# Attention in an eight-core transformer layer: the probability-times-value product, turned around and woven into the scores

## The reference

```python
x = x + attn(layernorm(x), ...)          # layernorm again inside, Wq, Wkv, Wout
#   q: 16 heads of 64, k and v: 4 groups of 64; q and k get a layernorm per head
#   attn = softmax(q k^T / 8); out = attn v; out @ Wout
x = x + ffn(layernorm(x), w1, w2)        # 1024 -> 4096 -> 1024, exact gelu,
#   ternary weights, activations quantized to 8 bits per token
```

## Time and profile before

| | |
|---|---|
| median of 3 runs | 9662.07 us (9659.97 to 9666.74) |
| profiled execution | 9662.5 us |
| its span on the slowest core (core 2) | 9661.0 us (all cores: 9604.8 to 9661.0) |
| TensorE busy | 4180.0 us, 43% |
| VectorE busy | 3207.8 us, 33% |
| ScalarE busy | 1954.3 us, 20% |
| mean granted TensorE clock | 0.595 |
| attention core of the two sequences | 1366.2 and 1367.0 us |

### The profile page before, as it was taken

The page is one execution under the profiler, slowest core; times in us unless marked ns, Lnnn a source line. Parts: engine busy times, 40 slices in busy tenths (PEclk is TensorE's granted clock), DMA queues, the critical chain, the costliest instruction groups (busy, mean ns, idle before and its releaser), DMA issues.

```text
span 9661.0 us, 60136 instructions; the slowest of 8 cores (9604.8 to 9661.0 us)
## 1 busy us (share of the span) xinstructions
PE 4180.0 (43%) x19456; PEld 1636.5 (17%) x19456; DVE 3207.8 (33%) x5038; ACT 1954.3 (20%) x2197; POOL 0.2 (0%) x4
## 2 busy tenths in 40 slices
PE   4233656666664365666665200222212222015445
PEld 0000211222221121222222100111101111002222
DVE  0423131111111322111111377655566555660000
ACT  1012203434342211434433111000000000001111
POOL 0000000000000000000000000000000000000000
PEclk8675755555556665555555555666556666557777
DMA  4232000000001100000000100111101111022221
GB/s 156 89 128 79 11 0 1 1 1 1 1 3 52 50 0 0 1 1 1 1 1 24 57 28 29 37 52 52 50 22 33 52 52 52 31 76 70 70 67 53
DMA packets 199070, 358.72 MB, mean 37 GB/s; under 512 B 23257, under 2 KB 154718, under 8 KB 194674
## 3 DMA queue, kind: packets, MB, share of 16 engines
q1 hardware_dynamic: 198770, 354.87, 11.3%
HBM read 279.29 MB, written 75.50 MB: 37 GB/s over the span
## 4 chain that ended last, share of the span: by engine, by line
PE 38%; DVE 30%; ACT 14%; issue 8%; DMA 6%; SPq 3%; DVEq 1%; ACTq 0%
ACT pslab L768 6%; PE ps_PV L778 6%; PE ps_S L757 5%; PE ps_F L1210 5%; PE ps_F L1086 4%; PE pss L267 3%; PE ps_qn L735 3%; PE ps_W L835 2%; DVE hflt L1138 2%; DVE htile L1133 2%; DVE hflt L1134 2%; DVE hflt L1136 2%; PE ps_mu L611 2%; DVE colmisc L1117 1%; DVE ao_tm L790 1%
## 5 line engine op out<-in xcount | busy, mean ns | idle before, releaser
L757 PE MATMUL ps_S<-qt,kt 65*128 65x512 bf16 x2048 | 985.2, 611 | 278.8 <-ACT pslab L768 242.3
L768 ACT ACTIVATE pslab<-ps_S 128x1024 bf16<-128x1024 f32 x1024 | 994.8, 1021 | 152.1 <-PE ps_S L757 150.2
L1149 PE MATMUL ps_trH<-s_idb,hqtm 128*128 128x128 bf16 x1024 | 129.5, 307 | 1541.1 <-DVE colmisc L1142 1439.4
L1210 PE MATMUL ps_F<-hqin,w2tb 128*128 128x512 bf16 x2048 | 499.3, 406 | 561.4 <-DMA f2xst<-scr_x 430.6
L788 DVE RECIPROCAL colmisc<-ps_PV 128x1 f32<-128x1 f32 x512 | 86.1, 168 | 1948.7 <-PE ps_PV L778 1948.7
L778 PE MATMUL ps_PV<-vaug,pslab 128*128 128x65 bf16 x8192 | 531.5, 242 | 453.2 <-DVE ao_tm L790 365.4
L778 PEld LDWEIGHTS ps_PV<-vaug,pslab 128*128 128x128 bf16 x8192 | 463.4, 129 | 568.7 <-issue 568.7
L267 PE MATMUL pss<-wab,s_onescolf 128*1 128x512 f32 x512 | 310.1, 756 | 544.4 <-ACT wab L247 407.1
L1086 PE MATMUL ps_F<-w1tb,yi_fm 128*128 128x512 bf16 x2048 | 462.0, 388 | 191.6 <-DMA w1tb<-scr_w1t 189.5
L1110 ACT ACT_TABLE_LOAD x32 | 41.1, 1283 | 2134.3 <-DVE hqfm L1157 1134.8
L1149 PEld LDWEIGHTS ps_trH<-s_idb,hqtm 128*128 128x128 bf16 x1024 | 99.1, 138 | 1573.3 <-issue 1573.3
(11 more groups left out here) (187 smaller groups left out, 4920.1 us busy)
## 6 DMA issues: line engine op xcount, KB each, us to landing
w1tb<-scr_w1t SPq DMA_DIRECT2D x512, 128.0 KB, 2.8
wst<-w1t SPq DMA_DIRECT2D x24, 2048.0 KB, 8.4
wst<-w2t SPq DMA_DIRECT2D x96, 512.0 KB, 3.3
xstage<-x SPq DMA_DIRECT2D x64, 512.0 KB, 3.5
scr_hq<-hqfm SPq DMA_DIRECT2D x256, 128.0 KB, 2.2
hqin<-scr_hq SPq DMA_DIRECT2D x256, 128.0 KB
scr_x<-x2asm SPq DMA_DIRECT2D x32, 512.0 KB, 2.9
f_xst<-scr_x SPq DMA_DIRECT2D x32, 512.0 KB, 3.2
```

Source lines behind the costliest of these rows:

```text
L757: ins = q.matmul(out=psS[kt % 2][:, 512 * s:512 * (s + 1)], lhsT=kt65[:, N * g + 128 * kt: N * g + 128 * (kt + 1)], rhs=qt65[hb][:, 1024 * ...
L768: sA.inc(q.activation(out=pslab[:, 1024 * kt:1024 * (kt + 1)], in_=psS[kt % 2][:], func=AF.Exp))
L1149: ins = q.transpose(out=pstr[:, 128 * j:128 * (j + 1)], in_=hqtm[:, 128 * hc:128 * (hc + 1)], identity=idb[:])
L1210: ins = q.matmul(out=psF[:, half:half + 512], lhsT=w2tb[:, 1024 * hc + 128 * dc: 1024 * hc + 128 * (dc + 1)], rhs=hqin[:, 512 * hc:512 * ( ...
```

## The change

The attention core computes the same product with the operands exchanged. The values (128 keys x 65) are the stationary operand and the exponentials of 1024 queries stream by, in two matmuls of 512 columns per step, into a new accumulator `psFM` of 65 x 1024 that adds up over the 16 steps. Its row 65 is the row sum. The output has features in partitions, so the transposes, `ao_tm` and `psTR` go. TensorE's order within a block is now scores of step kt, then the product of step kt - 2; `pslab` becomes a ring of four steps. New semaphores count the scores (`sS2`) and the exps (`sE`).

After a block, VectorE takes the reciprocal of the row sum, 2 instructions of 1 x 512 in one partition, and copies the 64 rows out (`aostg`), 2 instructions. The next block's first product waits for this (`evp`). SyncE writes the reciprocals to memory (`scr_rl`) and reads them back into 64 partitions (`rlb`), and VectorE multiplies by them one block later, into `ao_b`. `barrier` also waits for the new counts.

```diff
+    scr_rl = nc.dram_tensor("scr_rl", [2, 1024], F32).ap()
...
+    sS2 = Ctr(es.enter_context(nc.semaphore("sS2")))
+    sE = Ctr(es.enter_context(nc.semaphore("sE")))
...
                 if eng != "tensor":
                     q.wait_ge(sP.h, tp)
+                    q.wait_ge(sS2.h, ts2)
...
                 if eng != "scalar":
                     q.wait_ge(sA.h, ta)
+                    q.wait_ge(sE.h, te)
...
-    def attn_core_phase(b, pslab, ao_tm):
+    def attn_core_phase(b, pslab):
         st = ExitStack()
         psS = [st.enter_context(nc.psum_tensor(_u(f"ps_S{i}"), [128, 1024], F32)) for i in range(2)]
-        psPV = st.enter_context(nc.psum_tensor(_u("ps_PV"), [128, 65], F32))
+        psFM = st.enter_context(nc.psum_tensor(_u("ps_FM"), [65, 1024], F32))
         psn = st.enter_context(nc.psum_tensor(_u("ps_qn"), [65, 512], F32))
-        psTR = st.enter_context(nc.psum_tensor(_u("ps_aTR"), [128, 1024], BF16))
+        aostg = st.enter_context(nc.sbuf_tensor(_u("aostg"), [64, 2 * 1024], F32))
+        rlrow = st.enter_context(nc.sbuf_tensor(_u("rlrow"), [1, 2 * 1024], F32))
+        rlb = st.enter_context(nc.sbuf_tensor(_u("rlb"), [64, 2 * 1024], F32))
+        e0, s20 = sE.n, sS2.n
+
...
+        drain_rec = {-1: sV.n}
+        tt_rec = {-2: sV.n, -1: sV.n}
...
         for c in range(NC_D):
             g = c // 2
-            ba = sA.n
 
             @blk.scalar
-            def _(q, c=c, tgt=sP.n):
+            def _(q, c=c, tgt=psn_done_prev_c):
                 q.wait_ge(sP.h, tgt)
                 sA.inc(q.activation(out=qsq[:], in_=q_ln[:, N * c:N * (c + 1)], func=AF.Square))
+            sq_inc[c] = sA.n
 
             for hp in range(2):
                 hb = hp
 
                 @blk.vector
-                def _(q, c=c, hp=hp, hb=hb, tgt=sP.n):
-                    q.wait_ge(sP.h, tgt)
+                def _(q, c=c, hp=hp, hb=hb):
+                    if c > 0:
+                        q.wait_ge(sS2.h, s2v(4 * (c - 1) + 2 * hp + 1, 15))
                     sV.inc(q.tensor_scalar(out=qt65[hb][0:64, :],
...
                 for quarter in range(4):
-                    bv4 = sV.n
-
                     @blk.tensor
-                    def _(q, hp=hp, quarter=quarter, ba=ba, bv4=bv4):
-                        q.wait_ge(sA.h, ba + 1)
-                        q.wait_ge(sV.h, bv4)
+                    def _(q, c=c, hp=hp, quarter=quarter, tb=last_bias):
+                        q.wait_ge(sA.h, sq_inc[c])
+                        q.wait_ge(sV.h, tb)
...
+                    last_bias = sV.n
+                psn_last = sP.n
                 bvq = sV.n
 
                 for qb in range(2):
-                    bpS, baE = sP.n, sA.n
+                    i = 4 * c + 2 * hp + qb
+                    ph = i % 2
+                    coords[i] = (c, hp, qb)
+
+                    @blk.scalar
+                    def _(q, i=i):
+                        for kt in range(16):
+                            q.wait_ge(sS2.h, s2v(i, kt))
+                            gl = 16 * i + kt
+                            sE.inc(q.activation(
+                                out=pslab[:, 1024 * (gl % 4):1024 * (gl % 4 + 1)],
+                                in_=psS[kt % 2][:], func=AF.Exp))
 
                     @blk.tensor
-                    def _(q, g=g, hb=hb, qb=qb, bvq=bvq, baE=baE):
+                    def _(q, g=g, hb=hb, qb=qb, i=i, bvq=bvq, evp=drain_rec[i - 1]):
+                        def pv_pair(j):
+                            q.wait_ge(sE.h, exv(i, j))
+                            if j == 0:
+                                q.wait_ge(sV.h, evp)
+                            gl = 16 * i + j
+                            for s in range(2):
+                                ins = q.matmul(
+                                    out=psFM[:, 512 * s:512 * (s + 1)],
+                                    lhsT=vaug[:, 1040 * g + 65 * j: 1040 * g + 65 * (j + 1)],
+                                    rhs=pslab[:, 1024 * (gl % 4) + 512 * s:
+                                              1024 * (gl % 4) + 512 * (s + 1)],
+                                    start=(j == 0), stop=(j == 15))
+                            sP.inc(ins)
+
                         q.wait_ge(sV.h, bvq)
                         for kt in range(16):
-                            q.wait_ge(sA.h, baE + max(0, kt - 1))
+                            gprev = 16 * i + kt - 2
+                            if gprev >= 0:
+                                q.wait_ge(sE.h, e0 + gprev + 1)
                             for s in range(2):
                                 ins = q.matmul(
                                     out=psS[kt % 2][:, 512 * s:512 * (s + 1)],
                                     lhsT=kt65[:, N * g + 128 * kt: N * g + 128 * (kt + 1)],
                                     rhs=qt65[hb][:, 1024 * qb + 512 * s: 1024 * qb + 512 * (s + 1)],
                                     start=True, stop=True)
-                            sP.inc(ins)
-
...
-                    baE2 = sA.n
-
-                    for qt in range(8):
-                        @blk.tensor
-                        def _(q, g=g, qt=qt, baE2=baE2, tgtV=sV.n):
-                            q.wait_ge(sA.h, baE2)
-                            q.wait_ge(sV.h, tgtV)
-                            for kc in range(16):
-                                ins = q.matmul(
-                                    out=psPV[:],
-                                    lhsT=pslab[:, 1024 * kc + 128 * qt: 1024 * kc + 128 * (qt + 1)],
-                                    rhs=vaug[:, 1040 * g + 65 * kc: 1040 * g + 65 * (kc + 1)],
-                                    start=(kc == 0), stop=(kc == 15))
-                            sP.inc(ins)
-
+                            sS2.inc(ins)
+                            if kt >= 2:
+                                pv_pair(kt - 2)
+                        pv_pair(14)
+                        pv_pair(15)
+                    pv15[i] = sP.n
+
+                    @blk.vector
+                    def _(q, i=i, ph=ph):
+                        q.wait_ge(sP.h, pv15[i])
+                        if i >= 2:
+                            q.wait_ge(dRa.h, 16 * ra_rec[i - 2])
+                        for s in range(2):
+                            VS(q, q.reciprocal(
+                                out=rlrow[0:1, 1024 * ph + 512 * s:1024 * ph + 512 * (s + 1)],
+                                in_=psFM[64:65, 512 * s:512 * (s + 1)]))
+                        for s in range(2):
+                            sV.inc(q.tensor_copy(
+                                out=aostg[:, 1024 * ph + 512 * s:1024 * ph + 512 * (s + 1)],
+                                in_=psFM[0:64, 512 * s:512 * (s + 1)]))
+                    drain_rec[i] = sV.n
+
+                    @blk.sync
+                    def _(q, i=i, ph=ph):
+                        q.wait_ge(sV.h, drain_rec[i])
+                        if i >= 2:
+                            q.wait_ge(dRb.h, 16 * rb_rec[i - 2])
+                        dRa.inc(q.dma_start(out=scr_rl[ph:ph + 1, :],
+                                            in_=rlrow[0:1, 1024 * ph:1024 * (ph + 1)]))
+                        ra_rec[i] = dRa.n
+                        q.wait_ge(dRa.h, 16 * ra_rec[i])
+                        q.wait_ge(sV.h, tt_rec[i - 2])
+                        dRb.inc(q.dma_start(
+                            out=rlb[:, 1024 * ph:1024 * (ph + 1)],
+                            in_=scr_rl[ph:ph + 1, :].to_broadcast([64, 1024])))
+                        rb_rec[i] = dRb.n
+                        q.wait_ge(dRb.h, 16 * rb_rec[i])
+
+                    if i >= 1:
                         @blk.vector
-                        def _(q, hp=hp, qb=qb, qt=qt, tgt=sP.n):
-                            q.wait_ge(sP.h, tgt)
-                            VS(q, q.reciprocal(out=colmisc[:, 8:9], in_=psPV[:, 64:65]))
-                            qtg = 8 * qb + qt
-                            sV.inc(q.tensor_scalar(
-                                out=ao_tm[:, 128 * qtg + 64 * hp: 128 * qtg + 64 * (hp + 1)],
-                                in0=psPV[:, 0:64], scalar1=colmisc[:, 8:9],
-                                scalar2=None, op0=OP.mult))
-
-            for half in range(2):
-                @blk.tensor
-                def _(q, half=half, tgt=sV.n):
-                    q.wait_ge(sV.h, tgt)
...
+                        def _(q, i=i):
+                            ip = i - 1
+                            cp, hpp, qbp = coords[ip]
+                            php = ip % 2
+                            q.wait_ge(dRb.h, 16 * rb_rec[ip])
+                            sV.inc(q.tensor_tensor(
+                                out=ao_b[64 * hpp:64 * (hpp + 1),
+                                         N * cp + 1024 * qbp:N * cp + 1024 * (qbp + 1)],
+                                in0=aostg[:, 1024 * php:1024 * (php + 1)],
```

(37 more changed lines are left out.)

30 lines of the change are left out of this document (18 added, 12 removed).

## The result

| | before | after |
|---|---|---|
| median | 9651.01 us (8 runs, 9639.99 to 9666.74) | 9048.97 us (8 runs, 9012.44 to 9057.6) |
| profiled execution, its span | 9662.5, 9661.0 us | 9054.8, 9053.3 us (core 7; all cores 9008.9 to 9053.3) |
| ratio | | 0.9368 [0.9354, 0.9382] |

The change saves 602 us, 6.3%. The prediction was 9065 us, 16 above the median.

The account below looks back on a forecast made before the run. No engine was full: scores and exps alternated, then ScalarE slept through the products. Per sequence 15.35 + 16 x (20.45 + 25.05) + 15 x 20.6 + 15.5 = 1068 us against 1366.6, saving 597 over two: 9065 us, range 8660 to 9320.

Parts of the forecast that it names:

- the block after a bias stage: Attention core, first block of a pair, from its first score matmul to its last product: 20.45 us.
- the block after a block: Attention core, second block of a pair, from the previous block's last product to its own: 25.05 us.
- the bias stage: Ahead of each later pair of blocks, four rounds standing behind the drain on VectorE: 20.6 us.
- the first bias stage: Start of a sequence's attention core, ahead of its first block: 15.35 us.
- the end: End of a sequence, after its last block: drain 8.75, bare transfers 5.5 and multiply 1.2, together 15.5 us.
- the sequence: Attention core of one sequence, all blocks, bias stages and end: 1068 us, against 1366.6 before.
- The reciprocal: Drain after each block, VectorE's reciprocal of 512 elements in one partition: taken as 3.5 us, between 0.69 and 5.8.
- the rule that each microsecond costs 128 us: Drain: each microsecond of a reciprocal's time is paid 2 x 64 times, 128 us in all.
- The clock: TensorE in the attention core: rises from 1.2 to 2.4 GHz 5.1 us after steady work starts.
- The rival of a clock that stays at 1.2 GHz: Attention core: TensorE bounds every step at the low clock, total 9629 us with a 3.5 us reciprocal; chance 13%.
- Step 0.93 us by ScalarE: Attention core at the high clock: each step takes 0.93 us, with ScalarE the bound.
- The held-down level: Rival: TensorE held below full at 1.06 us a step in each block's warm steps, 83 us more, 9148; chance 5%.

Follow-up runs that it names:

- the second filler kernel: Changed kernel plus useless matmuls in each pair's second block, 9 behind the scores of step 1 and 20 behind those of step 2: 8959.55 us, ratio 0.9287.
- the kernel with the first of the two edits: Kernel with spread reciprocal and woven-in bias stage, plus the next block's first two score steps ahead of the last two products: 8183.37 us, ratio 0.8475.
- both edits: Kernel with spread reciprocal and woven-in bias stage, plus next block's first scores ahead of the last two products and one ScalarE program block: 8164.3 us, ratio 0.8452.

## Why the prediction was right

- **The steps of the sum.** Averaged over core 7, the block after a bias stage took 20.7 us (20.45 forecast; the one shown is 1562.59 - 1542.08 = 20.5), the block after a block 24.8 (25.05; the one shown took 25.6), the bias stage 20.1 (20.6), the first bias stage 15.1 (15.35), the end 15.2 (15.5), the sequence 1060 (1068). None of these is off by more than 2.5%.
- **The reciprocal** took 3.35 us against 3.5, from a span of 0.69 to 5.8 that one surplus of 10 ns set. The choice of half that surplus was a guess that fell well, and with it the total; the rule that each microsecond costs 128 us held (355 us for 2.67, so 133; 127 by the ratios). The Trainium skill (VectorE: DVE Perf Modes, First, the fixed hardware budget) led to 4.4 us; the measurement is a quarter below, so the estimate by its repeat count was too high here.
- **The clock** rose after steady work, as the earlier trace rows had it: after 3.8 us in one block shown and 5.6 in the next, where 5.1 was taken for both. Over the first blocks of all pairs on the eight cores it was 2.9 to 6.4 us, in most 4.6. It was 0.71 over the stretch. The rival of a clock that stays at 1.2 GHz fell. Why the clock was low in the second block is another matter: the prediction put it down to the wait of 5 us for the drain. In 173 of the 256 second blocks it was low with the first matmul behind the 2.1 us pause, ahead of that wait, and filling that wait alone did not keep it up. The price came out right because both pauses lie ahead of product 0, which is luck.
- **Step 0.93 us by ScalarE** in the late part of a block: 12 exps in a row take 11.85 us, the last of them 1.02, so (11.85 - 1.02)/11 = 0.98 a step; some of these steps took 1.05, at the level of 0.81.
- **The held-down level**, given 5%, did appear, on some cores and in some blocks; the forecast for it, 83 us, was several times too high, since it needs the level in all warm steps. The Trainium skill (TensorE: Matmul & The Clock Gate, Part 1) has that factor, 13/16 = 0.81, for a die on which three cores run dense matmuls; the traces agree with the level, and not with this condition, since the second filler kernel, with denser work on all cores, has 1 to 3 such pairs in a sequence.
- **What it didn't see**: how much of the gain needs no weave (half), and that the clock falls behind a pause of 2 us.

## What to carry to other kernels

Ask of each wait of TensorE not only how long it is, but at which clock the engine works behind it: here a fall behind a pause of 2.1 us cost some 3 us more (20.3 against 17.5 us for a block), and work placed in it, even useless work, paid for itself once every pause ahead of the block was filled. An operation that walks along one partition costs by its length there; spread it over partitions, even by way of memory, when something else runs meanwhile. A result that another block's first product waits for must leave its accumulator first and be finished later.

## What the runs showed of the hardware

- A reciprocal costs 3352 ns for 1x512 and 0.20 us for 128x8: the cost goes by the elements of one partition, 6.5 ns each, against 1.3 for a copy (685 ns for 1x512).
- TensorE's clock fell behind a pause of 2.1 us. With the accumulator released first it was low in 202 of 256 second blocks from the first matmul behind the pause, fell up to 2.1 us later in 42, and stayed up in 12; with copies for reciprocals it stayed up in 110. With the pause filled it never fell.
- A third level of 0.81 shows in woven steps, on some cores and not on others: on cores 4 and 5 of the kernel with the first of the two edits about 230 pairs in each sequence, with 1283 to 1284 us of attention core and spans of 8224 and 8220 us, against 1248 to 1250 and 8154 to 8170 on cores 0 to 3; with both edits 95 to 188 on cores 2 and 3 and at most 1 on the others. What triggers it was not settled.
- ScalarE loads its table at each new program block even though the function is the same, 1283 ns each; one program block for all exps had none of these. Of two such loads a pair of blocks paid for one.
